# Corner sums ahead of projections in the last tiles of a gather stage, with more corners on VectorE

## The chip, the cores and the metric

The kernel runs on one core of a Trainium2 chip. The metric is the device time of one execution in microseconds, as the median of several runs. Beside it stands one profiled execution, whose trace gives start and duration of each instruction.

## What is computed

The input is one image of 256 channels and 96x96 pixels. Two layers follow, each on a group-normalised input and each added to it. The first (a frequency filter, a query projection, a mask and a value projection) fills the first part of the run and isn't touched. The second is a deformable 1x1 convolution: each pixel has four learned offsets (heads), the projected image is sampled bilinearly at each of them, and the four samples are summed with softmax weights:

```python
proj = jnp.einsum('bchw,oc->bohw', x, Wc) + bc[None, :, None, None]
...
feats = jax.vmap(lambda g: grid_sample_bilinear_zeros(proj, g))(vgrid_scaled)
out = jnp.einsum('kbohw,bkhw->bohw', feats, weights)
```

Four heads with four bilinear corners each make 16 corners a pixel. Each is a row of 256 channels with a weight.

## The kernel before

The last stage, the gather stage, works on 72 tiles (`NT`) of 128 pixels, numbered 0 to 71, in 36 pairs (`PAIRS`); `LAST` is pair 35, with tiles 70 and 71. The kernel samples the unprojected image and projects the sum, so a tile goes through these steps:

- **Gather.** GpSimd issues an indirect DMA per tile and head (line 951), four a tile, each bringing the head's four corners for 128 pixels (four corners of 256 floats a pixel) into one of the buffers `places`. They are issued in order of tile and head.
- **Corner sum, shared.** `ON_DVE` says which corners VectorE adds, `ON_PE` which TensorE does. An even tile has 10 corners on VectorE and 6 on TensorE, an odd one 9 and 7. VectorE's `add(t, n)` (lines 1165 and 1168) multiplies a corner by its weight and adds it to a sum in PSUM; each addition of a tile waits for the one before. TensorE's `combine(t)` (line 1520) multiplies a corner by a diagonal of weights that ScalarE wrote before (`diags`, line 1308). A corner is two matmul records in the trace.
- **Join.** VectorE's `join(t)` (line 1175) adds TensorE's sum to VectorE's. It waits for `combine(t)` and for the last `add` of the tile.
- **Transpose and project.** TensorE turns the pair's sum (`transpose(p)`, line 1532), ScalarE copies it out of PSUM (`keep(p)`, line 1321), TensorE multiplies it by the 256x256 matrix and adds the bias (`project(p)`, lines 1544 and 1546), VectorE adds x (`result(p)`, line 1182), and SyncE stores 256 KB (line 898). The last pair does this tile by tile: `last_transpose(i)` (line 1556), a copy (line 1344), `last_project(i)` (lines 1571 and 1573), the last result (line 1213) and a store of 128 KB (line 903), with i = 0 for tile 70 and i = 1 for tile 71.

Each engine runs its own instructions strictly in the order in which they are written; semaphores tie the engines together. VectorE's additions stand in `TURNS`: turn t takes the additions of tile t-1 from the sixth on and the first five of tile t, one of each in turn. So the later part of a tile's additions is interleaved with the next tile's first ones, except in the turn after tile 71, where nothing is left to interleave.

The end of TensorE's order is written out by hand: `combine(68)`, `project(31)`, `combine(69)`, `project(32)`, `transpose(33)`, then these lines, where `LAST - 2` and `LAST - 1` are pairs 33 and 34 and `NT - 2` and `NT - 1` tiles 70 and 71:

```python
project(LAST - 2)
transpose(LAST - 1)
combine(NT - 2)
project(LAST - 1)
last_transpose(0)
combine(NT - 1)
last_project(0)
last_transpose(1)
last_project(1)
```

The end of VectorE's order is: turn 70, `join(69)`, `result(32)`, turn 71, `join(70)`, `result(33)`, turn 72 (the remaining additions of tile 71), `result(34)`, `join(71)`, the two last results. ScalarE's is: `keep(34)`, the four diagonals for the bias of pairs 34 and 35 (`diag_sums`, line 1314), the copies after the two last transposes.

Of the kernel before, what the change touches and what calls it, by code (L numbers as in the profile page):

```python
# [38 lines left out]
NT = HW // P  # L39
# [3 lines left out]
HEADS = 4  # L43
# [98 lines left out]
def build(nc, x, WqT, bq, WvT, bv, WpT, bp, out):  # L142
# [7 lines left out]
    with ExitStack() as ctx:  # L150
# [3 lines left out]
        def sem(name):  # L154
            return ctx.enter_context(nc.semaphore(name))
# [25 lines left out]
        def column(name, n=1):  # L181
            if name not in col:
                col[name] = (sum(w for _, w in col.values()), n)
            a, w = col[name]
            return small[:, a:a + w]
# [13 lines left out]
        with ExitStack() as c0:  # L199
# [449 lines left out]
            with ExitStack() as c3:  # L649
# [81 lines left out]

                PAIRS = NT // 2

                ON_DVE = [[(k, q) for k in range(HEADS) for q in range(n[k])] for n in ((3, 3, 2, 2), (3, 2, 2, 2))]
                ON_PE = [[(k, q) for k in range(HEADS) for q in range(4) if (k, q) not in mine] for mine in ON_DVE]
                ND = [len(mine) for mine in ON_DVE]
                NP = [len(mine) for mine in ON_PE]


                HALF = 5  # L740
                TURNS = []
                for t in range(NT + 1):
                    rest = [(t - 1, n) for n in range(HALF, ND[(t - 1) % 2])] if t > 0 else []
                    first = [(t, n) for n in range(HALF)] if t < NT else []
                    both = itertools.zip_longest(rest, first)
                    TURNS.append([a for two in both for a in two if a is not None])
# [53 lines left out]
                for t in range(NT):  # L800
                    if t in JOINS:
                        i = FIRST_DONE + JOINS.index(t) * CB
# [36 lines left out]
                added = sem("added")  # L839
# [21 lines left out]
                def added_by(t, n):  # L861

                    return PLACE[t, n] + 1

                def last_of_head(t, k):
                    return max(n for n, (head, _) in enumerate(ON_DVE[t % 2]) if head == k)

                def diags_by(t):

                    return (t // 2) * sum(NP) + sum(NP[:t % 2 + 1])  # L870

                with nc.Block(no_gpsimd_drain=True) as block:
                    @block.sync
# [83 lines left out]
                    def _(dve):  # L957
# [191 lines left out]

                        def add(t, n):  # L1150
                            p, i = t // 2, t % 2
                            k, q = ON_DVE[i][n]
                            if n == 0 or ON_DVE[i][n - 1][0] != k:
                                dve.wait_ge(landed[place_of[t, k]], 16 * use_of[t, k])
                            if n == ND[i] - 1:
                                if p >= 2:
                                    dve.wait_ge(turned, p - 1)
                                to = sums[p % 2][:, i, :]
                            else:
                                to = ps[:, DVE_SUM, i * C:(i + 1) * C]  # L1160
                            corner, weight = places[place_of[t, k]][:, q * C:(q + 1) * C], weights[:, t, k, q:q + 1]
                            if n == 0:
                                if p >= 1:
                                    dve.wait_ge(added, added_by(t - 2, ND[i] - 1))
                                V.tensor_scalar(to, corner, weight, None, ALU.mult).then_inc(added, 1)
                            else:
                                dve.wait_ge(added, added_by(t, n - 1))
                                V.scalar_tensor_tensor(to, corner, weight, ps[:, DVE_SUM, i * C:(i + 1) * C],  # L1168
                                                       ALU.mult, ALU.add).then_inc(added, 1)

                        def join(t):
                            p, i = t // 2, t % 2
                            dve.wait_ge(combined, t + 1)
                            dve.wait_ge(added, added_by(t, ND[i] - 1))
                            V.tensor_tensor(sums[p % 2][:, i, :], ps[:, PE_SUM[i], 0:C], sums[p % 2][:, i, :], ALU.add) \
                                .then_inc(joined, 1)

                        def result(p):

                            dve.wait_ge(projected, p + 1)  # L1180
                            here = xs[:, :, p * 2 * P:(p + 1) * 2 * P]
                            V.tensor_tensor(here, ps[:, PROJECT[p % 2], :].rearrange("p (c n) -> p c n", c=CB), here,  # L1182
                                            ALU.add).then_inc(out_ready, 1)
# [21 lines left out]
                                result(p - 3)  # L1205
                        for a in TURNS[NT]:
                            add(*a)
                        result(LAST - 1)
                        join(NT - 1)
                        for i in range(2):  # L1210
                            dve.wait_ge(projected, LAST + 1 + i)
                            here = xs[:, :, (NT - 2 + i) * P:(NT - 1 + i) * P]
# [4 lines left out]
                    def _(act):  # L1217
# [84 lines left out]
                        def diags(t):  # L1302
                            if t in FIRST:
                                act.wait_ge(weights_ready, GROUP_OF[t] + 1)
                            if t >= DIAGS:
                                act.wait_ge(combined, t - DIAGS + 1)
                            for n, (k, q) in enumerate(ON_PE[t % 2]):
                                S.activation(diag[t % DIAGS][n], ident[:, :], ACT.Copy, scale=weights[:, t, k, q:q + 1]) \  # L1308
                                    .then_inc(diag_ready, 1)

# [37 lines left out]
                    def _(pe):  # L1348
# [113 lines left out]
                        for n in range(NCH - LAG, NCH):  # L1462
# [4 lines left out]
                                 start=True, stop=True).then_inc(mean1_out, 1)  # L1467
# [29 lines left out]
                        for kb in range(CB):  # L1497
                            m = T.matmul(ps[:, flow_bank(0), 0:NFLOW], first_x[:, kb, :], wps[:, kb, HEADS_COLS], start=kb == 0,
                                         stop=kb == CB - 1)
# [11 lines left out]
                        def combine(t):  # L1511

                            i = t % 2
                            pe.wait_ge(diag_ready, diags_by(t))
                            if t >= 2:
                                pe.wait_ge(joined, t - 1)
                            for n, (k, q) in enumerate(ON_PE[i]):
                                if n == 0 or ON_PE[i][n - 1][0] != k:
                                    pe.wait_ge(landed[place_of[t, k]], 16 * use_of[t, k])
                                m = T.matmul(ps[:, PE_SUM[i], 0:C], diag[t % DIAGS][n], places[place_of[t, k]][:, q * C:(q + 1) * C],  # L1520
                                             start=n == 0, stop=n == NP[i] - 1)
                            m.then_inc(combined, 1)

                        def transpose(p):
# [10 lines left out]
                        def project(p):  # L1535

                            pe.wait_ge(sample_ready, p + 1)
                            if p >= 2:
                                pe.wait_ge(out_ready, p - 1)
                            pe.wait_ge(sum_ready, 2 * p + 2)  # L1540
                            for cb in range(CB):
                                o = ps[:, PROJECT[p % 2], cb * 2 * P:(cb + 1) * 2 * P]
                                for kb in range(CB):
                                    T.matmul(o, wps[:, kb, cb * P:(cb + 1) * P], sample[p % 2][:, kb, :], start=kb == 0, stop=False)  # L1544
                                for i in range(2):
                                    m = T.matmul(o[:, i * P:(i + 1) * P], bias[:, cb * P:(cb + 1) * P],  # L1546
                                                 diag_sum[(2 * p + i) % DIAGS], start=False, stop=i == 1)
                            m.then_inc(projected, 1)

                        def last_transpose(i):  # L1550

                            pe.wait_ge(joined, NT - 1 + i)
                            if i == 0:
                                pe.wait_ge(sample_ready, LAST - 1)
                            for cb in range(CB):
                                m = T.transpose(ps[:, LAST_TURNED[i], cb * P:(cb + 1) * P], sums[LAST % 2][:, i, cb * P:(cb + 1) * P],
                                                ident[:, :])
                            m.then_inc(turned, 1)
# [29 lines left out]
                                transpose(p - 1)  # L1588


                        project(LAST - 2)
                        transpose(LAST - 1)
                        combine(NT - 2)
                        project(LAST - 1)
                        last_transpose(0)
                        combine(NT - 1)
                        last_project(0)
                        last_transpose(1)
                        last_project(1)
# [28 lines left out]
```

## Time and profile before

| | us |
|---|---|
| median of 3 runs | 645.86 (645.61 to 646.09) |
| the profiled execution | 644.93 |
| its span, first to last instruction | 643.1 |
| TensorE busy in the span | 577.7 (90%) |
| VectorE busy | 548.8 (85%) |
| ScalarE busy | 349.2 (54%) |
| GpSimd busy | 383.2 (60%) |

The profiled execution took 0.93 us less than the median of the runs; 1.8 us of its time lie outside the span. All times below are us from the start of the span. Busy shares are means over stages with different limits, so for an edit of the last 20 us they say little: what counts is which wait ends last there.

### The profile page before, as it was taken

How to read it: one execution, taken by the hardware profiler on the slowest of the kernel's cores; microseconds unless marked ns; L12 is line 12 of the kernel's file. 1: busy time of each engine (PE TensorE's matmuls, PEld its weight loads, DVE VectorE, ACT ScalarE, POOL GpSimd, SP SyncE). 2: the span in 40 equal slices, each digit the busy share in tenths (PEclk: the TensorE clock that was granted, in tenths of full speed). 3: DMA queues.
4: the chain of work that ended last, by engine and by line, in shares of the span. 5: the costliest groups of instructions: out<-in, count | busy, mean ns of one | idle time of the engine just before them, and what ended most of it. 6: DMA issues, size and time to landing. Idle time of an engine off the chain costs nothing.

```text
span 643.1 us, 10845 instructions
## 1 busy us (share of the span) xinstructions
PE 577.7 (90%) x3022; PEld 467.8 (73%) x3030; DVE 548.8 (85%) x1336; ACT 349.2 (54%) x866; POOL 383.2 (60%) x387
## 2 busy tenths in 40 slices
PE   0579989999999975997999899999999999898987
PEld 0234467577887855986999799888878887786877
DVE  7899867457888987489997999899889989998894
ACT  0278887577877734435455455464554536455331
POOL 0040189023544465777777777777777777777770
PEclk9989999999999976597999999999999999999999
DMA  9920000213667577889999999999999999999882
GB/s 350 415 71 0 1 1 1 73 38 88 192 200 210 176 231 248 234 259 299 323 375 383 385 391 397 398 383 402 399 388 393 390 394 369 380 352 317 282 239 75
DMA packets 77377, 168.81 MB, mean 262 GB/s; under 512 B 14301, under 2 KB 43776, under 8 KB 77196
## 3 DMA queue, kind: packets, MB, share of 16 engines
q0 software_dynamic: 43488, 126.06, 54.8%
q1 hardware_dynamic: 33836, 42.13, 18.7%
q8 instruction: 23, 0.38, 0.2%
q14 instruction: 30, 0.25, 0.1%
HBM read 168.15 MB, written 28.51 MB: 306 GB/s over the span
## 4 chain that ended last, share of the span: by engine, by line
PE 46%; DVE 17%; DMA 7%; issue 6%; ACT 3%; POOL 2%; POOLq 0%; DVEq 0%; ACTq 0%
PE ps L1520 18%; PE ps L1389 9%; DVE ps L1168 8%; DMA v<-table,index 5%; PE ps L1544 5%; PE ps L1482 4%; PE ps L1546 2%; PE ps L1427 2%; PE ps L1372 2%; POOL xs L931 1%; ACT v L1308 1%; DMA more<-table,index 1%; PE ps L1532 1%; DVE v L1009 1%; DVE xs L1182 1%
## 5 line engine op out<-in xcount | busy, mean ns | idle before, releaser
L951 POOL DMA_INDIRECT v<-table,index x155 | 153.6, 991 | 52.5 <-DVE ps L1168 19.8
L1308 ACT ACTIVATE v<-ident,weights 128x128 f32<-128x128 f32 x468 | 140.4, 388 | 8.2 <-PE ps L1520 5.4
L1520 PE MATMUL ps<-v 128*128 128x256 f32 x520 | 128.3, 392 | 5.3 <-DMA v<-table,index 3.2
L1168 DVE SCALAR_TENSOR_TENSOR ps<-v,weights,ps 128x256 f32<-128x256 f32 x279 | 123.6, 481 | 0.7
L1520 PEld LDWEIGHTS ps<-v 128*128 128x128 f32 x520 | 97.8, 196 | 23.1 <-DMA v<-table,index 9.3
L931 POOL TENSOR_TENSOR xs<-xs,v 128x512 f32<-128x512 f32 x36 | 45.1, 1276 | 51.6 <-DVE v L1009 51.6
L1389 PE MATMUL ps<-wq,s_ring 128*128 128x256 f32 x288 | 68.0, 379 | 0.0
L951 POOL DMA_INDIRECT xs<-table,index x56 | 55.5, 990 | 17.1 <-issue 7.6
L1389 PEld LDWEIGHTS ps<-wq,s_ring 128*128 128x128 f32 x288 | 54.8, 190 | 9.6 <-issue 0.8
L1321 ACT COPY pick_mask<-ps 128x512 f32<-128x512 f32 x18 | 10.5, 586 | 86.6 <-PE ps L1532 86.6
L1168 DVE SCALAR_TENSOR_TENSOR ps<-xs,weights,ps 128x256 f32<-128x256 f32 x121 | 56.8, 482 | 0.6
L1321 ACT COPY sample<-ps 128x512 f32<-128x512 f32 x17 | 9.9, 585 | 87.1 <-PE ps L1532 87.1
L559 PE MATMUL ps<-xs,wvs 128*128 (+1 forms) x104 | 50.5, 647 | 5.7 <-ACT v L494 3.4
L488 ACT ACTIVATE a_ring<-xs,small 128x768 f32<-128x768 f32 (+1 forms) x48 | 49.0, 1024 | 9.2 <-POOL t_ring L475 5.2
L475 POOL TENSOR_SCALAR t_ring<-a_ring,small 128x768 f32<-128x768 f32 x24 | 31.8, 1335 | 36.5 <-DVEq L416 34.2
L559 PEld LDWEIGHTS ps<-xs,wvs 128*128 128x128 f32 x104 | 20.8, 206 | 33.8 <-issue 28.0
L1482 PEld LDWEIGHTS ps<-wps,xs 128*128 128x128 f32 x284 | 43.8, 230 | 2.0 <-issue 0.7
L1546 PEld LDWEIGHTS ps<-v,bias 128*128 128x128 f32 x280 | 42.3, 191 | 3.6
L1546 PE MATMUL ps<-v,bias 128*128 128x128 f32 x280 | 42.6, 275 | 0.0
L1520 PE MATMUL ps<-xs,v 128*128 128x256 f32 x150 | 39.5, 388 | 3.1 <-issue 1.8
L1482 PE MATMUL ps<-wps,xs 128*128 128x12 f32 x284 | 41.5, 281 | 0.0
L951 POOL DMA_INDIRECT more<-table,index x33 | 32.7, 990 | 10.1 <-issue 5.2
(196 smaller groups left out, 1174.9 us busy)
## 6 DMA issues: line engine op xcount, KB each, us to landing
table<-stage SPq DMA_DIRECT2D x72, 256.0 KB, 3.0
out_dram<-xs SPq DMA_DIRECT2D x35, 256.0 KB, 6.7
xs<-in_x_dram SPq DMA_DIRECT2D x11, 768.0 KB, 11.2
early<-const_syn POOLq DMA_DIRECT2D x18, 192.0 KB, 3.8
v<-table,index POOLq DMA_INDIRECT x155, 6.5
ana<-const_ana SPq DMA_DIRECT2D x1, 2304.0 KB, 20.1
xs<-table,index POOLq DMA_INDIRECT x56, 6.6
stage<-table,index POOLq DMA_INDIRECT x33, 6.3
```

Of the source, the lines that this page charges most:

```text
L475: nc.gpsimd.tensor_scalar(t_ring[u][:, :], a_ring[u][:, :], column("less_mn")[:, t:t + 1], column("sc")[:, t:t + 1], ALU.add, ALU.mult).th ...
L488: S.activation(a_ring[u][:, :], xs[:, t, ds(j * (2 * QCH) + u * QCH, QCH)], ACT.Abs, scale=column("rstd")[:, t:t + 1], bias=column("nmr")[ ...
L559: m = T.matmul(ps[:, bank, :], wvs[:, kb, ob * P:(ob + 1) * P], xs[:, kb, ds(chunk * CHUNK, CHUNK)], start=kb == 0, stop=kb == CB - 1)
L931: nc.gpsimd.tensor_tensor(xs[:, cb, here], xs[:, cb, here], v[:, cb, here], ALU.add) \
L951: nc.gpsimd.indirect_dma_start(places[a], None, table, bass.IndirectOffsetOnAxis(ap=index[:, t, k:k + 1], axis=0), bounds_check=HW + W - 1 ...
L1168: V.scalar_tensor_tensor(to, corner, weight, ps[:, DVE_SUM, i * C:(i + 1) * C], ALU.mult, ALU.add).then_inc(added, 1)
L1308: S.activation(diag[t % DIAGS][n], ident[:, :], ACT.Copy, scale=weights[:, t, k, q:q + 1]) \
L1389: m = T.matmul(o, s2_ring[n % 2][kb][:, i * P:(i + 1) * P], wq[:, kb, :], start=False, stop=kb == CB - 1, skip_group_check=True)
L1482: m = T.matmul(ps[:, flow_bank(g), i * NFLOW:(i + 1) * NFLOW], xs[:, kb, t * P:(t + 1) * P], wps[:, kb, C:NPROJ], start=kb == 0, stop=kb = ...
L1520: m = T.matmul(ps[:, PE_SUM[i], 0:C], diag[t % DIAGS][n], places[place_of[t, k]][:, q * C:(q + 1) * C], start=n == 0, stop=n == NP[i] - 1)
L1544: T.matmul(o, wps[:, kb, cb * P:(cb + 1) * P], sample[p % 2][:, kb, :], start=kb == 0, stop=False)
L1546: m = T.matmul(o[:, i * P:(i + 1) * P], bias[:, cb * P:(cb + 1) * P], diag_sum[(2 * p + i) % DIAGS], start=False, stop=i == 1)
```

## The change

The corner split becomes a matter of `kind(t)`: 0 and 1 for even and odd tiles as before, 2 and 3 for tiles 70 and 71. Of these VectorE adds 12 and 11 corners (before: 10 and 9) and TensorE 4 and 5 (before: 6 and 7). In tile 70 each head gives its last corner to TensorE; in tile 71 the heads give one, one, one and two.

On TensorE `combine(70)` moves ahead of `project(33)`, and `combine(71)` and `last_transpose(0)` ahead of `project(34)`. On VectorE `join(71)` moves ahead of `result(34)`. ScalarE writes 4 and 5 diagonals for the two tiles, before 6 and 7. Nothing else changes.

```diff
+                BY_HEAD = ((3, 3, 2, 2), (3, 2, 2, 2), (3, 3, 3, 3), (3, 3, 3, 2))
+
+                def kind(t):
+                    return t % 2 + (2 if t >= NT - 2 else 0)
+
+                ON_DVE = [[(k, q) for k in range(HEADS) for q in range(n[k])] for n in BY_HEAD]
...
-                    rest = [(t - 1, n) for n in range(HALF, ND[(t - 1) % 2])] if t > 0 else []
+                    rest = [(t - 1, n) for n in range(HALF, ND[kind(t - 1)])] if t > 0 else []
...
                         for a in TURNS[NT]:
                             add(*a)
+                        join(NT - 1)
                         result(LAST - 1)
-                        join(NT - 1)
...
-                            for n, (k, q) in enumerate(ON_PE[t % 2]):
+                            for n, (k, q) in enumerate(ON_PE[kind(t)]):
...
+                        combine(NT - 2)
                         project(LAST - 2)
                         transpose(LAST - 1)
-                        combine(NT - 2)
+                        combine(NT - 1)
+                        last_transpose(0)
                         project(LAST - 1)
-                        last_transpose(0)
-                        combine(NT - 1)
                         last_project(0)
                         last_transpose(1)
                         last_project(1)
```

The other lines of the diff put `kind(t)` where a count of corners was taken by `t % 2`.

## Rows read from the trace of the kernel before

**Rows 1.** Page, 40 slices of the span: TensorE's granted clock, in tenths.

```profile
PEclk9989999999999976597999999999999999999999
```

**Rows 2.** Chain that ended last, in order of time: start us, us, what.

```profile
623.11 0.45 PE ps L1532 x4
...
624.06 0.70 ACT v L1314 x2
...
633.62 3.02 PE ps L1520 x14
...
640.30 0.42 DVE xs L1213
```

**Rows 3.** Timeline of TensorE: start us, us, engine, line, operation, out<-in, count, idle time before.

```profile
622.94 0.60 PE L1532 MATMUL ps<-ident,wvs 128*128 128x128 f32 x4
624.90 1.10 PE L1544 MATMUL ps<-sample,wps 128*128 128x256 f32 x4 [1.35 <-ACT v L1314]
625.84 0.61 PE L1546 MATMUL ps<-v,bias 128*128 128x128 f32 x4
...
628.03 2.76 PE L1520 MATMUL ps<-xs,v 128*128 128x256 f32 x12
630.62 1.03 PE L1544 MATMUL ps<-pick_mask,wps 128*128 128x256 f32 x4
...
633.24 0.38 PE L1556 MATMUL ps<-ident,wvs 128*128 128x128 f32 x2
633.46 1.46 PE L1520 MATMUL ps<-xs,v 128*128 128x256 f32 x6
...
636.48 0.61 PE L1571 MATMUL ps<-sample,wps 128*128 128x128 f32 x4
...
637.82 0.38 PE L1556 MATMUL ps<-ident,wvs 128*128 128x128 f32 x2
```

**Rows 4.** The same of VectorE.

```profile
628.33 0.47 DVE L1168 SCALAR_TENSOR_TENSOR wvs<-xs,weights,ps 128x256 f32<-128x256 f32 x1
628.72 0.48 DVE L1168 SCALAR_TENSOR_TENSOR ps<-xs,weights,ps 128x256 f32<-128x256 f32 x1
630.82 0.42 DVE L1175 TENSOR_TENSOR wvs<-ps,wvs 128x256 f32<-128x256 f32 x1 [1.62 <-PE ps L1520]
631.16 0.68 DVE L1182 TENSOR_TENSOR xs<-ps,xs 128x512 f32<-128x512 f32 x1
631.76 1.00 DVE L1168 SCALAR_TENSOR_TENSOR ps<-early,weights,ps 128x256 f32<-128x256 f32 x2
632.87 0.49 DVE L1168 SCALAR_TENSOR_TENSOR ps<-v,weights,ps 128x256 f32<-128x256 f32 x1
633.46 0.48 DVE L1168 SCALAR_TENSOR_TENSOR wvs<-v,weights,ps 128x256 f32<-128x256 f32 x1
```

**Rows 5.** Line 951, GpSimd's gathers, 615 to 620 us: tile 70's four, one before.

```profile
L951 POOL DMA_INDIRECT xs<-table,index x4: 986/988/990, 615.6 to 619.5; - x4
...
DMA to landing us min/median/max: 3.7/4.8/5.1
```

**Rows 6.** The same of tile 71's head 3, alone in its window.

```profile
L951 POOL DMA_INDIRECT v<-table,index x1: 990/990/990, 624.7 to 624.7; - x1
...
DMA to landing us min/median/max: 5.1/5.1/5.1
```

**Rows 7.** The same of all gathers of the run.

```profile
DMA to landing us min/median/max: 3.7/6.6/8.4
```

**Rows 8.** Busy time in stretches: A:B length, PE, PEld, DVE, ACT, POOL busy (x count), PEclk, DMA share, GB/s; two stores.

```profile
635.00:636.00 1.00, 1.00 (x6) 0.90 (x5) 0.00 (x0) 0.00 (x0) 0.00 (x0) 1.00 0.53 180
636.00:637.00 1.00, 1.00 (x8) 0.92 (x8) 0.32 (x1) 0.00 (x0) 0.00 (x0) 1.00 0.25 82
...
out_dram<-xs SPq DMA_DIRECT2D x1, 256.0 KB, 4.7
...
out_dram<-xs SPq DMA_DIRECT2D x1, 128.0 KB, 1.8
```

More of the change, by code:

```diff
@@ L732, in build @@
                 PAIRS = NT // 2
-                ON_DVE = [[(k, q) for k in range(HEADS) for q in range(n[k])] for n in ((3, 3, 2, 2), (3, 2, 2, 2))]
+                BY_HEAD = ((3, 3, 2, 2), (3, 2, 2, 2), (3, 3, 3, 3), (3, 3, 3, 2))
+                def kind(t):
+                    return t % 2 + (2 if t >= NT - 2 else 0)
+                ON_DVE = [[(k, q) for k in range(HEADS) for q in range(n[k])] for n in BY_HEAD]
                 ON_PE = [[(k, q) for k in range(HEADS) for q in range(4) if (k, q) not in mine] for mine in ON_DVE]
@@ L865, in last_of_head @@
                 def last_of_head(t, k):
-                    return max(n for n, (head, _) in enumerate(ON_DVE[t % 2]) if head == k)
+                    return max(n for n, (head, _) in enumerate(ON_DVE[kind(t)]) if head == k)
                 def diags_by(t):
-                    return (t // 2) * sum(NP) + sum(NP[:t % 2 + 1])
+                    return sum(NP[kind(i)] for i in range(t + 1))
                 with nc.Block(no_gpsimd_drain=True) as block:
@@ L1151, in add @@
                             p, i = t // 2, t % 2
-                            k, q = ON_DVE[i][n]
-                            if n == 0 or ON_DVE[i][n - 1][0] != k:
+                            mine = ON_DVE[kind(t)]
+                            k, q = mine[n]
+                            if n == 0 or mine[n - 1][0] != k:
                                 dve.wait_ge(landed[place_of[t, k]], 16 * use_of[t, k])
-                            if n == ND[i] - 1:
+                            if n == len(mine) - 1:
                                 if p >= 2:
@@ L1163, in add @@
                                 if p >= 1:
-                                    dve.wait_ge(added, added_by(t - 2, ND[i] - 1))
+                                    dve.wait_ge(added, added_by(t - 2, ND[kind(t - 2)] - 1))
                                 V.tensor_scalar(to, corner, weight, None, ALU.mult).then_inc(added, 1)
@@ L1173, in join @@
                             dve.wait_ge(combined, t + 1)
-                            dve.wait_ge(added, added_by(t, ND[i] - 1))
+                            dve.wait_ge(added, added_by(t, ND[kind(t)] - 1))
                             V.tensor_tensor(sums[p % 2][:, i, :], ps[:, PE_SUM[i], 0:C], sums[p % 2][:, i, :], ALU.add) \
@@ L1516, in combine @@
                                 pe.wait_ge(joined, t - 1)
-                            for n, (k, q) in enumerate(ON_PE[i]):
-                                if n == 0 or ON_PE[i][n - 1][0] != k:
+                            mine = ON_PE[kind(t)]
+                            for n, (k, q) in enumerate(mine):
+                                if n == 0 or mine[n - 1][0] != k:
                                     pe.wait_ge(landed[place_of[t, k]], 16 * use_of[t, k])
                                 m = T.matmul(ps[:, PE_SUM[i], 0:C], diag[t % DIAGS][n], places[place_of[t, k]][:, q * C:(q + 1) * C],
-                                             start=n == 0, stop=n == NP[i] - 1)
+                                             start=n == 0, stop=n == len(mine) - 1)
                             m.then_inc(combined, 1)
```

## Prediction

> **What bounds the kernel now.** The edit touches only what follows the corner sums of tile 69, so I read the end of the run. First the page: TensorE's granted clock is full in the last 21 of the 40 slices, so all costs below are at the upper of its two levels, 2.4 GHz [rows 1]. Then the chain that ended last: in the last 20 us it is TensorE almost throughout: `transpose(33)`, a short leg over ScalarE, `project(33)`, `combine(70)`, `project(34)`, `combine(71)` (3.02 us), `last_project(0)`, `last_transpose(1)`, a copy, `last_project(1)` and the last addition [rows 2]. Then TensorE's timeline for holes. There is one of 1.35 us before `project(33)` at 624.90, which waits for ScalarE's bias diagonals [rows 2, 3]; the next work, tile 70's corners, stood behind it in the queue. Last VectorE's timeline: `join(70)` idles 1.62 us for TensorE, so VectorE has room there [rows 4].
>
> The gathers are no limit at the end. Four of tile 70 start 1.3 us apart up to 619.5, and the window that holds them shows no landing over 5.1 us, so head 3 is in by 624.6 [rows 5]. Head 3 of tile 71 starts at 624.7 and lands 5.1 us later, at 629.8 [rows 6]; TensorE uses it only in the last four records of `combine(71)`, ten records of 0.216 us behind 633.46, so at 635.6 and 5.8 us later [rows 3].
>
> **The sum, TensorE.** I count starts. A corner is two records, and 12 records take 630.62 - 628.03 = 2.59 us, so 0.432 us a corner [rows 3].
> 1. `transpose(33)` starts at 622.94 and takes 0.45 us [rows 2], so `combine(70)` can start at 623.39. Its fourth corner comes up at 624.69, just after its gather (624.6), and it ends at 625.12.
> 2. `project(33)` starts there and not at 624.90. Its first four matmuls took 0.94 us after the hole and take about 0.86 in a row (633.24 - 630.62 = 2.62 for the whole projection). Its fifth instruction comes at 625.98, before at 625.84: 0.14 late. So 2.59 us of corners leave the path and 0.14 come back: a gain of 2.45.
> 3. `transpose(34)` ends at 628.17 (628.03 + 0.14). Three corners of `combine(71)` take 1.30, to 629.47. The two of head 3 wait for the gather, to 629.80: 0.33 of new idle. Four matmuls of this width after a wait took 0.94 us (624.90 to 625.84), so they are through at 630.74.
> 4. `last_transpose(0)` takes 0.22 (633.46 - 633.24), to 630.96, if `join(70)` is done. `project(34)` takes 2.62, to 633.58; `last_project(0)` 637.82 - 636.48 = 1.34, to 634.92 [rows 3]. Then `last_transpose(1)`, which started at 637.82. By TensorE alone the gain is 2.90 us: the hole filled (1.51 by starts, 623.39 to 624.90), four corners moved away (1.73), less 0.33 of idle; one slow restart goes and one comes.
>
> **The sum, VectorE.** Independent additions start 0.39 us apart (628.33, 628.72). In a chain where each waits for the last it is 0.52 (631.76, two in 1.00, less 0.48), and 0.59 where the instruction has a second wait as well (to 632.87, to 633.46) [rows 4]. That is a price for the additions: 0.59 for a head's first, for a tile's last and for the join, 0.52 for others.
> 1. Turn 71 has two more additions. Eleventh and twelfth of tile 70 come after 628.72, at 629.11 and 629.70; `join(70)` at 630.29, done at 630.71. It no longer waits for TensorE, and TensorE wants it at 630.74: a tie.
> 2. `result(33)` comes 0.34 later and turn 72 another 0.60 (630.82, 631.16, 631.76): 631.23. Six additions, each dependent: 0.59 + 0.52 + 0.52 + 0.59 + 0.59 bring the last to 634.04, `join(71)` starts at 634.63 and is done at 635.05. TensorE wants it at 634.92. So VectorE decides by 0.15, and `last_transpose(1)` starts at 635.07.
> 3. `result(34)` stands behind `join(71)`: 634.97, done at 635.6. Who waits for it: the last result of tile 70 (its projection is done by then) and SyncE's stores. The two last additions aren't delayed, since tile 71's comes 2.48 us after `last_transpose(1)` (637.82 to 640.30), at 637.55 [rows 2, 3].
>
> So 637.82 - 635.07 = **2.75 us gained**.
>
> The Trainium skill (VectorE: DVE Perf Modes, section The DRAIN you can't avoid) says the opposite of my price for chains: a semaphore after each operation costs nothing over one after the last. By that rule all steps would be 0.39, `join(71)` would be done near 633.6, and TensorE's 2.90 would stand. The trace disagrees (0.52 and 0.59 against 0.39), and I keep the trace's.
>
> **Edits at nothing.** Four diagonals fewer on ScalarE: it idles there, and this saves nothing. `last_transpose(0)` ahead of `project(34)`: its copy hides beneath the projection. GpSimd: no gather waits for tile 70 or 71, so it issues as before. Bank reuse: `last_project(0)` needs `result(33)`, out by about 631.3, and starts at 633.6.
>
> **Stores.** The three last ones would be issued at the ends of the three last VectorE results: near 635.6 (634.97 and 0.68), 636.0 and 638.0. A 256 KB store kept the DMA engines busy for 0.53 + 0.25 = 0.78 us, and the last 128 KB took 1.8 us to land [rows 8]. By share the first two need 1.2 us and are out of the way before 638; so nothing, at most 0.3.
>
> **Bounds.** The chain price is between 0.39 (gain 2.90) and, if eight dependent steps cost 0.07 more than I take, 0.56 worse (gain 2.2). The gather between 3.7 us (no more gain, as VectorE then decides) and the run's median of 6.6 [rows 7].
>
> **Rivals.**
> - **The last gather takes the path** (0.12). Before it had 5.8 us to spare, now it has none, and each us of lateness moves all of TensorE's end. At 6.6 us, the median of all gathers, it lands 1.5 later, `last_transpose(1)` starts at 636.42 and the gain is 1.4: 644.5 [rows 7]. For it: the whole stage's landings. Against: up to 629.8 no transfer starts earlier or later than now, and the window before shows 5.1 at most [rows 5].
> - **Slower, by the same queue order** (0.03). TensorE stands at tile 71's head 3 with `project(34)` behind it. From a landing 2.9 us later, 8.0 us after its start, the order loses. The longest of the run is 8.4 [rows 7]: `last_transpose(1)` at 638.22, 0.4 lost, 646.3. The four latest gathers are well under that, with fewer of them under way.
> - **The hole isn't filled** (0.03), so that the reordering doesn't do what it says: tile 70's head 3 lands 1.4 us late, `combine(70)` ends at 626.5 and not at 625.12. Then `combine(71)` finds its last gather landed, and its five corners end at 628.17 + 1.35 + 2.16 = 631.68, 0.94 later: a gain of 2.0, 643.9. Against: head 3 has 0.1 us in hand, and its gather is upstream of all that changes.
> - **The last store takes it back** (0.05). If it queues behind the other two and takes 4.7 us, as a store did beside gathers, and not 1.8 [rows 8], 2.9 us come back: 646.0, no difference. Against: no gather runs then, and the 1.2 us of transfer above fit in before it.
> - **More than forecast** (0.03): 3.0 us or over, 642.7, if `join` needs less than 0.59 and the last gather lands early.
>
> **How the numbers follow.** The profiled execution would go from 644.93 to 642.2 and its span from 643.1 to 640.35. The median of the runs, 645.86, is 0.93 above the profiled one; I take 2.75 off it: **643.1 us**. The forecast, a gain of 2.2 to 3.0 (642.9 to 643.7), has 0.74. With the runs' own spread of 0.25 to each side, and reaching into the gather's case, the range is 642.4 to 644.2. A measurement of this kernel tells about 0.2%, 1.3 us, from no change: faster is below 644.57. Faster are the forecast, the larger gain, the unfilled hole and half of the gather's case: 0.86. Same are its other half and the store's case: 0.11. Slower: 0.03.
>
> **What would show it.** Right: no hole before `project(33)`, which starts near 625.1; line 1520 waits some 0.3 us for the last gather near 629.8; `join(70)` with no wait for TensorE; the last six additions 0.52 to 0.59 apart, the join near 634.6; `last_transpose(1)` near 635.1; the last addition near 637.6. Wrong: a longer wait of line 1520 for a gather, a join over 0.5 us late, or a last store over 2.1 us to land.

## The result and the profile after

The changed kernel takes 643.45 us (median of 7 runs, 642.07 to 644.62) and the kernel before 645.86 (7 runs, 645.18 to 646.63). The ratio is 0.9962 with a 95% interval of 0.9951 to 0.9972: 2.4 us less, between 1.8 and 3.2. A second, later comparison gives 0.996 (0.9946 to 0.9975), 643.0 (9 runs) against 645.5 (14 runs, of which one took 988.72 us at a granted clock of 0.565 and isn't counted in the ratio).

| | before | after | forecast |
|---|---|---|---|
| median of the runs, us | 645.86 | 643.45 | 643.1 |
| profiled execution | 644.93 | 642.07 | 642.2 |
| its span | 643.1 | 640.3 | 640.35 |
| start of `transpose(33)`, called T below | 622.94 | 623.40 | 622.94 |
| start of `last_transpose(1)` | 637.82 | 634.96 | 635.07 |
| the last addition on VectorE | 640.30 | 637.45 | 637.55 |

In the changed file lines are 6 to 8 higher: 1528 is the corner sum on TensorE (before 1520), 1552 and 1554 the projection, 1540 and 1564 the transposes, 1579 and 1581 the last projection; 1172 and 1175 the additions on VectorE, 1182 the join, 1189 and 1220 the results; 957 the gathers.

TensorE's timeline of the changed kernel (start us, us, engine, line, operation, out<-in, count, and idle time before it, where there is one) answers [rows 3]:

```profile
623.40 0.60 PE L1540 MATMUL ps<-ident,wvs 128*128 128x128 f32 x4
623.84 1.89 PE L1528 MATMUL ps<-xs,v 128*128 128x256 f32 x8
625.57 1.03 PE L1552 MATMUL ps<-sample,wps 128*128 128x256 f32 x4
...
628.62 1.03 PE L1528 MATMUL ps<-xs,v 128*128 128x256 f32 x4
629.49 0.59 PE L1528 MATMUL ps<-early,v 128*128 128x256 f32 x2
629.92 1.03 PE L1528 MATMUL ps<-v 128*128 128x256 f32 x4
630.78 0.38 PE L1564 MATMUL ps<-ident,wvs 128*128 128x128 f32 x2
631.00 1.03 PE L1552 MATMUL ps<-pick_mask,wps 128*128 128x256 f32 x4
...
634.96 0.38 PE L1564 MATMUL ps<-ident,wvs 128*128 128x128 f32 x2
635.80 0.71 PE L1579 MATMUL ps<-sample,wps 128*128 128x128 f32 x4 [0.46 <-ACT sample L1351]
```

From 623.40 to 635.2 no line has an idle time: the hole before the projection is gone, and the four records of tile 71's head 3 (629.92) start without a wait. VectorE's timeline answers [rows 4]:

```profile
625.14 0.49 DVE L1172 TENSOR_SCALAR ps<-xs,weights 128x256 f32<-128x256 f32 x1 [0.46 <-DMA xs<-table,index]
625.54 3.61 DVE L1175 SCALAR_TENSOR_TENSOR ps<-xs,weights,ps 128x256 f32<-128x256 f32 x9
629.26 0.48 DVE L1175 SCALAR_TENSOR_TENSOR wvs<-xs,weights,ps 128x256 f32<-128x256 f32 x1
629.84 0.42 DVE L1182 TENSOR_TENSOR wvs<-ps,wvs 128x256 f32<-128x256 f32 x1
630.18 0.68 DVE L1189 TENSOR_TENSOR xs<-ps,xs 128x512 f32<-128x512 f32 x1
630.78 0.48 DVE L1175 SCALAR_TENSOR_TENSOR ps<-xs,weights,ps 128x256 f32<-128x256 f32 x1
631.36 1.54 DVE L1175 SCALAR_TENSOR_TENSOR ps<-early,weights,ps 128x256 f32<-128x256 f32 x3
633.01 0.49 DVE L1175 SCALAR_TENSOR_TENSOR ps<-v,weights,ps 128x256 f32<-128x256 f32 x1
633.60 0.48 DVE L1175 SCALAR_TENSOR_TENSOR wvs<-v,weights,ps 128x256 f32<-128x256 f32 x1
634.18 0.42 DVE L1182 TENSOR_TENSOR wvs<-ps,wvs 128x256 f32<-128x256 f32 x1
```

`join(70)` (629.84) waits for nothing. The chain of turn 72 takes 634.18 - 630.78 = 3.40 us from its first addition to the join, as forecast to the hundredth (631.23 to 634.63). It ends at 634.60, 0.36 before TensorE wants it.

### The profile page after: what moved, and what is told of

It reads as the page before. It is cut to its first block, busy times and chain, and to the rows that moved or that the text cites. A ratio compares the mean times of both kernels' runs of the same rounds, so it can differ in the third digit from the quotient of the medians.

```text
span 640.3 us, 10829 instructions
## 1 busy us (share of the span) xinstructions
PE 574.8 (90%) x3014; PEld 466.3 (73%) x3022; DVE 550.4 (86%) x1340; ACT 348.0 (54%) x862; POOL 384.0 (60%) x387
## 4 chain that ended last, share of the span: by engine, by line
PE 48%; DVE 15%; DMA 7%; issue 6%; ACT 3%; POOL 3%; POOLq 0%; DVEq 0%; ACTq 0%
PE ps L1528 18%; PE ps L1396 9%; DVE ps L1175 6%; PE ps L1552 5%; PE ps L1489 5%; DMA v<-table,index 4%; PE ps L1554 3%; PE ps L1434 2%; DMA more<-table,index 2%; PE ps L1379 2%; ACT v L1315 1%; POOL xs L937 1%; DMA xs<-table,index 1%; PE ps L1540 1%; DVE v L1015 1%
## 5 line engine op out<-in xcount | busy, mean ns | idle before, releaser
L1175 DVE SCALAR_TENSOR_TENSOR ps<-xs,weights,ps 128x256 f32<-128x256 f32 x124 | 58.1, 483 | 0.6
L1528 PE MATMUL ps<-xs,v 128*128 128x256 f32 x144 | 37.8, 386 | 4.3 <-DMA xs<-table,index 2.1
L957 POOL DMA_INDIRECT stage<-table,index x33 | 32.7, 992 | 10.1 <-DVE ps L1175 4.6
```

Source lines behind the costliest of these rows:

```text
L957: nc.gpsimd.indirect_dma_start(places[a], None, table, bass.IndirectOffsetOnAxis(ap=index[:, t, k:k + 1], axis=0), bounds_check=HW + W - 1 ...
```

## The experiments

**How they are read.** The chips of the first eight runs take 737 us for the kernel before and not 646, with runs from 731 to 743, so their times can't show one or two us. (One of them gave 0.9905 for a kernel that the trace shows to gain less than the changed one.) So I count from T in each trace: the matmuls behind it keep their 0.216 us on these chips too, and the kernel before has `last_transpose(1)` at T + 14.88 on both kinds (637.82 - 622.94, and 736.47 - 721.59 in a run below). The changed kernel has it at T + 11.56. VectorE doesn't start at a fixed distance from T. L says how far behind T its turn 71 begins: it is the start of tile 71's first addition, less 0.39 for the addition ahead of it in the turn, less T. It was 2.25 in the profile before and 1.35 after. In both of these that addition waited for tile 71's head 0, in the profile before for 1.03 us:

```profile
625.58 0.49 DVE L1165 TENSOR_SCALAR ps<-xs,weights 128x256 f32<-128x256 f32 x1 [1.03 <-DMA xs<-table,index]
```

In the first eight traces it waits for nothing.

**The order alone.** The old split in the new order.

```diff
-BY_HEAD = ((3, 3, 2, 2), (3, 2, 2, 2), (3, 3, 3, 3), (3, 3, 3, 2))
+BY_HEAD = ((3, 3, 2, 2), (3, 2, 2, 2), (3, 3, 2, 2), (3, 2, 2, 2))
```

> The changed kernel's order on TensorE and VectorE, with the old split of corners (10 and 9 on VectorE) in tiles 70 and 71. My theory: the order alone fills the hole of 1.5 us before project(33), and TensorE is the limit to the end: last_transpose(1) 1.6 us earlier than before when counted from transpose(33), no wait for the last gather, since seven corners come up later; 644.3 us beside a before of 645.9, so two fifths to a half of the gain. Rival (the order is worth nothing without the lighter sums, because the longer sums put back what the hole gives): 645.9. Rival (the order is everything): 643.4.

TensorE's timeline, T at 710.48:

```profile
710.48 0.60 PE L1540 MATMUL ps<-ident,wvs 128*128 128x128 f32 x4
710.92 2.76 PE L1528 MATMUL ps<-xs,v 128*128 128x256 f32 x12
713.51 1.03 PE L1552 MATMUL ps<-sample,wps 128*128 128x256 f32 x4
...
723.77 0.38 PE L1564 MATMUL ps<-ident,wvs 128*128 128x128 f32 x2
```

T + 13.29: 1.59 us gained, no hole. Time: 0.9967 (0.9936 to 0.9999) of before.

**The split alone.** The new split in the old order, on TensorE and VectorE.

> The new split (12 and 11 corners on VectorE) in the old order on both engines. My theory: four corners of 0.432 us leave TensorE, the hole of 1.35 us before project(33) stays, VectorE is not the limit: a gain of 1.7 us, 644.1 beside 645.9. If order and split add up, this and the order alone come to 3.3, of which the changed kernel shows 2.4 to 2.9. Rival (VectorE's longer chain of additions takes it back): gain under 0.8, join(71) then starts after combine(71) has long ended.

TensorE's timeline, T at 710.00:

```profile
710.00 0.60 PE L1540 MATMUL ps<-ident,wvs 128*128 128x128 f32 x4
711.96 1.10 PE L1552 MATMUL ps<-sample,wps 128*128 128x256 f32 x4 [1.36 <-DVE xs L1189]
...
715.09 1.89 PE L1528 MATMUL ps<-xs,v 128*128 128x256 f32 x8
...
723.15 0.38 PE L1564 MATMUL ps<-ident,wvs 128*128 128x128 f32 x2
```

The hole is there, 1.36 us. (The profile names VectorE's result as what ended it; that result ended at 711.84, ScalarE's diagonals at 711.81.) `last_transpose(1)` is at T + 13.15: 1.73 gained, four corners of 0.432. Time: 0.9985 (0.9951 to 1.002). The two parts, 1.59 and 1.73, make 3.32, which is the changed kernel's whole 14.88 - 11.56: the parts simply add as long as TensorE is the limit.

**The first move alone.** `combine(71)` and `last_transpose(0)` go back behind `project(34)`.

```diff
+project(LAST - 1)
+last_transpose(0)
 combine(NT - 1)
-last_transpose(0)
-project(LAST - 1)
```

> The changed kernel, but combine(71) and last_transpose(0) stay behind project(34); only combine(70) is moved ahead. My theory: the first hole is filled, but project(34) now stands right behind transpose(34) and waits for ScalarE's copy and bias diagonals, a new hole of some 1.5 us, which combine(71) covers in the changed kernel. last_transpose(1) 1.1 us later than in the changed kernel: 644.1 beside 645.9, no wait for the last gather. Rival (the moved combine(71) brings nothing, or costs, by its wait for the last gather): as fast as the changed kernel or faster, 643.4 or less.

TensorE's timeline behind `transpose(34)`:

```profile
722.91 0.60 PE L1540 MATMUL ps<-ident,wq 128*128 128x128 f32 x4
724.87 1.10 PE L1552 MATMUL ps<-pick_mask,wps 128*128 128x256 f32 x4 [1.36 <-ACT v L1321]
```

T is 718.12 and `last_transpose(1)` starts at 731.27, T + 13.15: 1.6 us behind T + 11.56, half a us more than expected. (L is 2.01 here. By the rule found below, L + 9.88 where VectorE is the limit, the changed kernel would be at T + 11.89 and the loss 1.26.) The hole has not gone, it has moved to the next projection, for the same reason: a projection right behind its own transpose waits for ScalarE's copy and bias diagonals. In the kernel before `combine(70)` covers that place. So `combine(71)` has to move because `combine(70)` did. The first move by itself is worth nothing: with the same split and no move at all, above, `last_transpose(1)` stood at T + 13.15 as well. The second move by itself wasn't run. Time: 1.0003 (0.9969 to 1.0036).

**VectorE's join behind the result again.**

```diff
-join(NT - 1)
 result(LAST - 1)
+join(NT - 1)
```

> The changed kernel with VectorE's join(71) behind result(34) again. Theory A (VectorE decides the start of last_transpose(1), as predicted): 0.3 to 0.4 us later than the changed kernel, the join behind an addition of 0.6 us. Theory B (TensorE decides, with VectorE 0.36 us ahead in the profile of the changed kernel): 0.1 to 0.3 us later, about 643.6 beside 645.9. Both say that the move is worth under 0.5 us; if it is worth more, the order of VectorE carries more than I think.

Measured: `last_transpose(1)` waits for the join, at T + 12.25 (T 715.91), 0.69 later than in the changed kernel's first profile and more than either theory said. Both had taken L as fixed: here it is 1.94, 1.35 in that profile, so VectorE's chain is late to begin with. Counted from VectorE's start it is L + 10.31, 0.43 over the L + 9.88 that the changed kernel has where VectorE is the limit (measured below as L + 9.90, twice). That is what the result ahead of the join costs. Time: 0.9969 (0.993 to 1.0008).

**One corner more, one corner fewer.** (4, 3, 3, 3) and (3, 3, 3, 3), then (3, 3, 3, 2) and (3, 3, 2, 2), for the last two entries of `BY_HEAD`.

> The changed kernel with one more corner of tile 70 and of tile 71 on VectorE (13 and 12; TensorE 3 and 4). Theory (chains of dependent additions cost 0.52 to 0.59 us a step, so VectorE becomes the limit): two more dependent additions, join(71) 1.05 us later than in the changed kernel's profile, at 635.65 where TensorE would be free from 634.1; last_transpose(1) 0.7 us later than 634.96: 644.1 beside 645.9. Rival (a step costs 0.39, a semaphore nothing, as the Trainium skill's page VectorE: DVE Perf Modes says in its section on the DRAIN): two steps 0.78 later, last_transpose(1) 0.4 later or less.

With 13 and 12 corners L is 2.96 (T 714.60) and VectorE holds TensorE at both joins, as TensorE's timeline shows:

```profile
723.65 0.44 PE L1564 MATMUL ps<-ident,wvs 128*128 128x128 f32 x2 [2.07 <-DVE wvs L1182]
...
728.51 0.44 PE L1564 MATMUL ps<-ident,wvs 128*128 128x128 f32 x2 [0.46 <-DVE wvs L1182]
```

T + 13.91, that is L + 10.95. Two more dependent additions cost 1.07 over L + 9.88, as expected from 0.52 and more a step, and not 0.78. What the Trainium skill says (VectorE: DVE Perf Modes, section The DRAIN you can't avoid), that a semaphore after each operation costs nothing extra, was measured there with `tensor_copy`. It gives no price for this chain: every addition here posts a semaphore, the independent ones too, and those start 0.39 apart all the same. The dearer steps are those that wait for the addition directly ahead.

> The changed kernel with one corner fewer of each tile on VectorE (11 and 10; TensorE 5 and 6). Theory (TensorE is the limit and 12 and 11 lie at the balance): two corners of 0.432 us more on TensorE, last_transpose(1) 0.86 us later when the last gather is in time: 644.3 beside 645.9. Rival (VectorE is the limit in the changed kernel): the same or faster.

Times of the two: 0.9905 (0.9868 to 0.9942) and 0.9946 (0.9921 to 0.9971). With 11 and 10 (T 722.00, L 2.89) `last_transpose(1)` starts at 734.42, T + 12.42, 0.86 behind T + 11.56: two corners on TensorE, with no wait anywhere. But at the same L the changed kernel would, by the rule, be at 2.89 + 9.88 = 12.77. So neither theory is right for all executions: which split is better depends on L, and by the rule 12 and 11 beat 11 and 10 only for L under 2.5. No run has the two side by side at one L.

**The last gather later, by memsets.**

```diff
+if (t, k) == (NT - 1, HEADS - 1):
+    for i in range(10):
+        nc.gpsimd.memset(pad[:, :], 0.0).then_inc(pad_done, 1)
+        pool.wait_ge(pad_done, i + 1)
```

> The changed kernel with a chain of small memsets on GpSimd (about 2.5 to 4 us, d in the following) ahead of the last gather, tile 71's head 3, which then lands d later. Theory (the new order leaves this gather 0.2 us to spare): TensorE waits in combine(71) with project(34) behind it, and the end is d - 0.3 us later: at d = 3 last_transpose(1) at 637.7 and 646.1 us, no faster than before. Rival (the gather has room as before): no change.

> The kernel before with the same memsets ahead of its last gather. Theory: the gather has 5.8 us to spare there, TensorE has all of project(34) between, so d of 2.5 to 4 us costs under 0.2 us: 645.9. VectorE's last two additions come later but the join waits for TensorE anyway (2.1 us). Rival (late traffic costs by itself, through the memsets or collisions with stores): later by much of d, and then the run beside it says nothing about the order.

Both say nothing about the gather's slack. On these chips the last gather starts 38 us before the end of the span (687.15 of 725.5) and a delay of 3.4 us (687.15 against 682.41 and the usual 1.30) is nothing. The changed kernel has T + 12.46 at L 2.56 (T 707.73), so L + 9.90, the kernel before 736.47 - 721.59 = T + 14.88, as ever. Times: 0.9953 (0.9912 to 0.9993) and 0.9973 (0.9939 to 1.0008).

**The changed kernel again**, on a chip where the kernel before takes 645.5.

> The changed kernel itself, on the chip of these four runs. I count from the start of transpose(33), T, and call L the start of VectorE's turn 71 counted from T (without waits for gathers). The eight traces so far fit one rule for the changed kernel's last_transpose(1): at T + 11.56 where TensorE is the limit, at T + L + 9.88 where VectorE is, the later of the two; the kernel before has T + 14.88. So it is to be 2.3 to 3.3 us earlier than before for L of 1 to 2.7. Rival (the tail isn't set by these two alone): a start more than 0.2 us off the rule.

TensorE's timeline, T at 625.05:

```profile
631.57 1.03 PE L1528 MATMUL ps<-v 128*128 128x256 f32 x4
632.92 0.44 PE L1564 MATMUL ps<-ident,wvs 128*128 128x128 f32 x2 [0.33 <-DVE wvs L1182]
...
637.26 0.44 PE L1564 MATMUL ps<-ident,wvs 128*128 128x128 f32 x2
```

VectorE's timeline of the same run:

```profile
627.75 0.49 DVE L1172 TENSOR_SCALAR ps<-xs,weights 128x256 f32<-128x256 f32 x1 [0.61 <-DMA xs<-table,index]
...
636.78 0.42 DVE L1182 TENSOR_TENSOR wvs<-ps,wvs 128x256 f32<-128x256 f32 x1
```

Tile 71's head 0 came late for VectorE, L is 2.31, and `last_transpose(1)` starts at T + 12.21 where the rule gives 12.19. Here VectorE decides: it holds TensorE for 0.33 us at the join of tile 70 and is done with tile 71's at 637.20, where TensorE alone would be at T + 11.56, 636.61. Most of that is the first of the two joins. `last_transpose(0)` stands at T + 7.87 here and at T + 7.38 in the first profile, 0.49 later, and from there TensorE's own work lasts till 637.16; tile 71's join adds the rest.

**The last gather held by a gate.** The gather waits for `transpose(34)` in both orders, so that it comes at the same place of either kernel.

```diff
+if (t, k) == (NT - 1, HEADS - 1):
+    pool.wait_ge(turned, LAST)
```

> The changed kernel, with the last gather (tile 71, head 3) issued only when transpose(34) is done, so that it starts near T + 5.5 and lands 3.7 to 5.1 us later, whatever the chip's gathers do: near T + 9.5. Theory: the new order needs it at T + 6.5, TensorE stands in combine(71) with project(34) behind it, and last_transpose(1) starts 5.1 us after the landing, near T + 14.6: nearly all of the gain is gone. Rival (the wait is absorbed, as the projection or VectorE fill in): T + 11.6 to 12.8.

> The kernel before with the same gate on its last gather. Theory: its order needs the gather at T + 12.7, three us after it lands, so last_transpose(1) stays at T + 14.9 and the order before is nearly insensitive. Rival (the late gather costs this order as well): T + 16 or later.

TensorE's timeline in the changed order, T at 623.36:

```profile
629.45 0.59 PE L1530 MATMUL ps<-early,v 128*128 128x256 f32 x2
633.28 1.13 PE L1530 MATMUL ps<-v 128*128 128x256 f32 x4 [3.24 <-DMA v<-table,index]
...
638.42 0.38 PE L1566 MATMUL ps<-ident,wvs 128*128 128x128 f32 x2
```

The same in the order before, T at 623.31:

```profile
635.98 1.03 PE L1522 MATMUL ps<-v 128*128 128x256 f32 x4
...
638.18 0.38 PE L1558 MATMUL ps<-ident,wvs 128*128 128x128 f32 x2
```

The gather lands near 633.2 and 633.6. The changed order stands 3.24 us for it and has `last_transpose(1)` at T + 15.06; TensorE doesn't notice in the order before, at T + 14.87. So the new order has spent the slack that the old one had for its last gather, and with a gather at T + 9.9 the whole gain is lost, with 0.2 us on top. The expected T + 14.6 counted on a start at T + 5.5; the gather started at 629.51, T + 6.15. The times of the two profiled executions, the only ones taken, are 645.50 and 645.25.

**A version that goes on.** Turn 71 takes tile 71's first seven additions, and `last_transpose(1)` stands between the halves of `last_project(0)`.

```diff
-first = [(t, n) for n in range(HALF)] if t < NT else []
+first = [(t, n) for n in range(HALF + 2 if t == NT - 1 else HALF)] if t < NT else []
...
+                                if between and cb == 0:
+                                    between()
...
-last_project(0)
-last_transpose(1)
+last_project(0, lambda: last_transpose(1))
```

The rest of the turn begins at the same count.

> A version that goes on from the changed kernel: tile 71's first seven additions and not five stand in turn 71, where they interleave with tile 70's, so that turn 72 is a chain of four dependent additions and not six; and last_transpose(1) stands between the two halves of last_project(0), so that ScalarE's copy hides beneath the second half. By the rule: the first instruction of last_project(1) starts at T + 11.8 where the changed kernel has T + 12.4 (L under 1.6), at T + L + 10.3 where the changed kernel has T + L + 10.8. So 0.5 to 0.6 us better than the changed kernel, which the times (some us of scatter) will not show; the trace will. Rival (the join of tile 70, 0.4 us later, takes it back by delaying last_transpose(0)): no earlier than the changed kernel by the same count.

TensorE's timeline:

```profile
632.71 0.44 PE L1568 MATMUL ps<-ident,wvs 128*128 128x128 f32 x2 [0.59 <-DVE wvs L1186]
...
636.27 0.38 PE L1568 MATMUL ps<-ident,wvs 128*128 128x128 f32 x2
636.49 0.61 PE L1583 MATMUL ps<-sample,wps 128*128 128x128 f32 x4
636.94 0.39 PE L1585 MATMUL ps<-v,bias 128*128 128x128 f32 x2
637.16 0.67 PE L1583 MATMUL ps<-sample,wps 128*128 128x128 f32 x4
```

T is 624.58 and L 2.17. `last_project(1)` starts at 637.16, L + 10.41. In the profile of the changed kernel on the same chip it starts at 638.16, L + 10.80. So 0.39 us better, less than the 0.5 to 0.6 expected: ScalarE's copy is hidden (no idle time before 637.16), but the rival has its part. `last_transpose(0)` waits 0.59 for the join of tile 70 and starts at L + 5.96, in the changed kernel at L + 5.56; behind it TensorE has no idle time, so this first join alone decides. Times: 642.68 (5 runs), 0.9948 (0.9932 to 0.9965) of before, against 0.996 (0.9946 to 0.9975) for the changed kernel. The two intervals overlap; that it is faster than the changed kernel is shown by the trace alone.

## Why the prediction was right, point by point

- **The hole** (TensorE, steps 1 and 2). Right. It is filled, and the order is worth 1.59 us. What the sum didn't say is that the second move is needed for the gain: with the first alone the hole of 1.36 us comes back one projection later.
- **Four corners** (TensorE, steps 3 and 4). Right: 1.73 us by the split alone.
- **0.33 us of idle for the last gather** (TensorE, step 3). Wrong: it didn't occur in either profile of the changed kernel. In the first the gather starts at 624.9 and lands 4.8 us later, at 629.7, and is wanted at 629.92; in the second it lands at about 631.1 and is wanted at 631.57. So 0.2 and 0.5 us were to spare. The forecast had kept the 5.1 us of one execution, and had held T at its old place to the hundredth. The rival built on the same wait has the right mechanism and price: 5.1 us from landing to `last_transpose(1)` forecast, 5.2 with the gate (633.2 to 638.42). It has not come up by itself.
- **The price of the chain** (VectorE). Right: 3.40 us from turn 72's start to the join, exactly; 1.07 for two additions more.
- **VectorE decides by 0.15** (VectorE, step 2). Wrong in the first profile of the changed kernel, where TensorE decides by 0.36, right in the second, where VectorE does by 0.65. The sum carried one execution's L. With its 2.25 the later rule gives T + 12.13 and so the forecast's 635.07; L was 1.35 and 2.31 in the two profiles of the changed kernel on chips of the faster kind. "The gathers are no limit at the end" was read from TensorE's and the last gather's rows alone. In the profile before, in the changed kernel's two and in that of the version that goes on, VectorE's turn 71 waits for tile 71's head 0, which takes 4.8, 4.1, 5.0 and 5.0 us from its issue to the addition. So a gather's flight sets L, and by it which engine decides.
- **Why it came out right in sum.** In the profiled execution TensorE gained 3.32 us from T on and T was 0.46 late: 2.86, forecast 2.75. That the two agree so closely is luck: a wait that didn't come and an engine that didn't decide would have made the gain 0.57 larger, and T's shift took most of it back. In the second profile T was at 625.05, 2.11 later than before, and `last_transpose(1)` only 0.56 earlier than in the profile before. T moves with the gathers ahead of it: in the six profiles from the faster kind of chip tile 71's head 2 is issued between 623.37 and 625.33, and T stands 0.11 to 0.43 ahead of that. The edit touches none of these gathers; with 622.94 and 623.31 for the old order against 623.36 to 625.05 for the new, the profiles are too few to show that it leaves T alone. From T on the gain is 14.88 less the larger of 11.56 and L + 9.88: 3.3 down to 2.7 for the L of the two profiles. The medians give 2.4 and 2.5. What the remaining tenths are, wider L or T, the runs' times can't tell.
- **Nothing from the stores, ScalarE and GpSimd.** Right. The last store lands in 1.8 us as before and the two ahead of it in 2.2 each, before in 2.1 and 1.8; from the last addition's start to the end of the span it is 2.85 us, before 2.80.

The stores of the changed kernel from 634 us on (KB each, us to landing):

```profile
out_dram<-xs SPq DMA_DIRECT2D x1, 256.0 KB, 2.2
...
out_dram<-xs SPq DMA_DIRECT2D x1, 128.0 KB, 2.2
out_dram<-xs SPq DMA_DIRECT2D x1, 128.0 KB, 1.8
```

## What to carry to other kernels

A hole on the busiest engine before a step that waits for a helper's copy is filled by work from behind it in the queue, but the step that leaves its place uncovers the next such wait: move the pair or nothing. When two engines meet at joins, write the end as the larger of two sums, each from its own start, and look how far those starts lie apart over several executions before saying which decides. Look too at what each start waits for: here it was a gather. An order that leaves the last transfer no slack can be priced by holding that transfer at a fixed point of both orders.

## What the runs showed of the hardware

An addition on VectorE whose input in PSUM is the one before's output starts 0.52 to 0.59 us after it, an independent one 0.39 (1.54 us for three against 3.61 for nine). So, by these rows, interleaving two tiles' sums is worth 0.13 to 0.2 us an addition, and the version that goes on used it.

The first eight runs came from chips where the same kernel takes 14% longer, all of it in the gather stage (the first gather starts at 252.6 us there and at 252.9 in the profile before). The busy time by stretches (length; busy time of TensorE, its weight loads, VectorE, ScalarE and GpSimd; granted clock, DMA share, GB/s) of the order alone there:

```profile
500.00:540.00 40.00, 31.01 (x148) 25.86 (x147) 25.62 (x70) 15.99 (x52) 26.73 (x27) 0.88 0.95 343
```

The same stretch of the changed kernel's profile:

```profile
500.00:540.00 40.00, 37.68 (x200) 31.41 (x199) 34.72 (x93) 20.79 (x68) 30.55 (x32) 1.00 1.02 386
```

The DMA engines are nearly as busy (0.95 against 1.02) and move 343 GB/s against 386. TensorE is busy 31.01 us against 37.68, and its granted clock stands at 0.88 on the mean; in the trace of the first move alone it was 0.50, the lower of its two levels, from 688.6 to 692.6. The last gather starts 45 us before the end there (684.24 of 729.1) and 15 us in the changed kernel's profile (624.89 of 640.3), so the end of the run is free of gathers. Why these chips move less, no run here shows.
